# Attention block on one core: DVE's and TensorE's first tiles reordered, image work put ahead of the maxima, six stores issued from ACT's queue

## The reference

```
h    = group_norm(x, 32 groups of 4 channels) * gamma + beta      # (C, N)
q, k, v = w_qkv @ h + b_qkv                                       # each (C, N)
attn = softmax(q^T k / sqrt(C))                                   # (N, N)
out  = x + w_proj @ (attn @ v)^T + b_proj
```

## Time and profile before

| | |
|---|---|
| Median of 3 runs | 129.59 us (128.44 to 129.79) |
| The profiled execution | 127.29 us |
| Its span in the trace | 125.5 us |
| TensorE (PE) busy | 114.0 us, 91% |
| DVE busy | 96.1 us, 77% |
| ACT busy | 90.8 us, 72% |
| POOL busy | 87.4 us, 70% |
| Granted clock of TensorE | 0.999 of full |
| Data moved by DMA | 20.66 MB in 67,728 packets |

### The profile page before, as it was taken

One profiled execution on the slowest core, in us unless ns is written; L12 is line 12 of the kernel. 1 busy time (PEld: TensorE's weight loads), 2 busy tenths in 40 slices (PEclk: granted clock), 3 DMA queues, 4 the chain that ended last, 5 costly groups with the idle time before them and its releaser, 6 DMA issues.

```text
span 125.5 us, 3198 instructions
## 1 busy us (share of the span) xinstructions
PE 114.0 (91%) x1193; PEld 79.2 (63%) x1193; DVE 96.1 (77%) x240; ACT 90.8 (72%) x126; POOL 87.4 (70%) x73
## 2 busy tenths in 40 slices
PE   5987976869999999999999999999999999998981
PEld 2442544547767777666656776776567867776970
DVE  3688799999776967988669579775695887776832
ACT  3039499499987878777897878878878788788200
POOL 2054079489999998999759988998666666766000
PEclk9999999999999999999999999999999999999999
DMA  4594007968889998999999999999999999999602
GB/s 112 140 341 161 0 4 133 174 116 166 167 60 205 194 179 145 239 193 190 132 261 195 140 202 235 193 139 213 214 173 124 208 230 196 123 209 227 168 5 84
DMA packets 67728, 20.66 MB, mean 165 GB/s; under 512 B 65409, under 2 KB 66177, under 8 KB 67713
## 3 DMA queue, kind: packets, MB, share of 16 engines
q1 hardware_dynamic: 67280, 20.46, 87.2%
q10 hardware_dynamic: 432, 0.00, 0.2%
HBM read 2.36 MB, written 2.10 MB: 36 GB/s over the span
## 4 chain that ended last, share of the span: by engine, by line
PE 71%; DVE 10%; POOL 6%; issue 4%; DMA 4%; ACT 3%; POOLq 0%; DVEq 0%
PE scores L743 10%; PE o_ps L761 10%; PE scores L745 10%; PE scores L744 10%; PE o_ps L769 10%; PE o_ps L762 9%; DVE row_max L539 4%; DMA ptT<-p_hl 4%; POOL p_hl L342 3%; PE scores L787 3%; PE o_ps L782 2%; DVE t_lo L527 2%; ACT z_hi L406 1%; PE misc L728 1%; PE misc L727 1%
## 5 line engine op out<-in xcount | busy, mean ns | idle before, releaser
L342 POOL TENSOR_TENSOR p_hl<-probs,p_hl 128x1024 f16<-128x1024 f32 x31 | 66.1, 2135 | 13.7 <-ACT p_hl L432 13.6
L539 DVE TENSOR_REDUCE row_max<-scores 128x1 f32<-128x1024 f32 x32 | 39.1, 1221 | 17.2 <-PE scores L745 17.0
L425 ACT ACTIVATE probs<-scores,exp_bias,esc 128x1024 f32<-128x1024 f32 x32 | 38.5, 1203 | 14.6 <-DVE exp_bias L544 14.6
L432 ACT ACTIVATE p_hl<-probs 128x1024 f16<-128x1024 f32 x32 | 33.8, 1057 | 1.0
L761 PE MATMUL o_ps<-v_hi,ptT 128*128 128x128 f16 x256 | 32.0, 219 | 1.7 <-issue 1.3
L762 PE MATMUL o_ps<-v_lo,ptT 128*128 128x128 f16 x256 | 32.0, 219 | 0.0
L761 PEld LDWEIGHTS o_ps<-v_hi,ptT 128*128 128x128 f16 x256 | 24.9, 98 | 8.2 <-issue 6.0
L743 PE MATMUL scores<-z_hi,t_hi 128*128 128x512 f16 x64 | 24.3, 379 | 2.6 <-ACT probs L425 1.7
L762 PEld LDWEIGHTS o_ps<-v_lo,ptT 128*128 128x128 f16 x256 | 25.0, 98 | 2.3
L745 PE MATMUL scores<-z_hi,t_lo 128*128 128x512 f16 x64 | 24.2, 379 | 0.0
L744 PE MATMUL scores<-z_lo,t_hi 128*128 128x512 f16 x64 | 24.2, 379 | 0.0
(11 more groups left out here) (134 smaller groups left out, 138.4 us busy)
## 6 DMA issues: line engine op xcount, KB each, us to landing
out_dram<-out_sb SPq DMA_DIRECT2D x7, 256.0 KB, 2.6
x_sb<-in_x_dram SPq DMA_DIRECT2D x3, 512.0 KB, 4.5
ptT<-p_hl SPq DMA_TRANSPOSE x61, 3.4
x_sb<-in_x_dram SPq DMA_DIRECT2D x2, 256.0 KB, 3.2
out_dram<-out_sb SPq DMA_DIRECT2D x1, 192.0 KB, 2.0
wqkv_sb<-in_L_conv_w_qkv_dram SPq DMA_DIRECT2D x1, 128.0 KB, 3.7
wp_sb<-in_L_conv_w_proj_dram SPq DMA_DIRECT2D x1, 64.0 KB, 3.4
wqkv_sb<-in_L_conv_w_qkv_dram SPq DMA_DIRECT2D x1, 64.0 KB, 3.1
```

The source lines that it names most:

```text
L342: nc.gpsimd.tensor_tensor(p_hl[:, g % RING, 1], probs[:, g % RING], p_hl[:, g % RING, 0], ALU.subtract).then_inc(plo_ready, 1)
L425: nc.scalar.activation(probs[:, g % RING], scores[:, g % SLOTS], ACT.Exp, bias=exp_bias[:, g:g + 1], scale=esc[:], accum_out=row_sum[:, g: ...
L432: nc.scalar.activation(p_hl[:, g % RING, 0], probs[:, g % RING], ACT.Copy).then_inc(phi_ready, 1)
L539: nc.vector.tensor_reduce(row_max[:, g:g + 1], scores[:, g % SLOTS], AX_X, ALU.max).then_inc(max_ready, 1)
```

## The change

The computation stays the same. The edits:

1. `store` becomes a helper with the queue as an argument. The six stores of tiles 0 to 23 are issued by ACT, in its loop behind `p_high(g)` at g = 9, 13, ..., 29. SP keeps the transposes and the last three stores.
2. `score_tile` at the first tile of an image waits for `thi_ready` first and for `tlo_ready` only ahead of the first matmul that reads `t_lo`.
3. Tile 0: on DVE `w_max` and `w_inv` come ahead of `t_low(0, 1)`, on TensorE the matmul for `w_max` comes ahead of `t_products(0, 1)`.
4. The copy to `ident16` moves from tile 2 to the prologue, ahead of the wait for gamma.
5. Image 1: `group_mean(1)` moves on DVE ahead of maxima(3), `group_var(1)` and `v_low(0, ...)` behind it; `normalise(1, ...)` on POOL and `z_high(1, ...)` on ACT move one tile later, from tiles 2 and 3 to 3 and 4. Statistics of image 2: `channel_stats` at tiles 4 and 5, TensorE's `group_mean(2)` at tile 6.
6. On DVE `t_low(b, 1)`, `v_low`, `channel_stats`, `group_mean`, `group_var` of the later images stand ahead of the maxima; `t_low(b + 1, 0)` stands directly behind the maxima of the image's last tile.
7. `v_products` and `v_high` of images 1 to 3 run at tiles s = 0 and 1 instead of 1 and 2. `values` waits for each half of `v_lo` only where it first reads it.

```diff
--- before.py
+++ after.py
@@ -251,6 +251,12 @@
 
         block = ctx.enter_context(nc.Block())
 
+        def store(queue, first, tiles):
+            b, s = divmod(first, TILES)
+            queue.wait_ge(out_ready, first + tiles)
+            queue.dma_start(out_d[b, :, s * P:(s + tiles) * P],
+                            out_sb[:, first * P:(first + tiles) * P]).then_inc(stored, 16)
+
         @block.sync
         def _(sp):
             w_d = w_qkv.rearrange("(t o) c -> o t c", t=3)
@@ -266,12 +272,6 @@
             for b in range(1, B):
                 sp.dma_start(x_sb[:, b * N:(b + 1) * N], x_d[b]).then_inc(x_rest[b - 1], 16)
 
-            def store(first, tiles):
-                b, s = divmod(first, TILES)
-                sp.wait_ge(out_ready, first + tiles)
-                sp.dma_start(out_d[b, :, s * P:(s + tiles) * P],
-                             out_sb[:, first * P:(first + tiles) * P]).then_inc(stored, 16)
-
             for g in range(G):
 
                 wait(sp, pv_ready, g - PT_RING + 1)
@@ -283,13 +283,9 @@
                     sp.wait_ge(plo_ready, g + 1)
                     sp.dma_start(ptT[:, g % PT_RING, 1], p_hl[:, g % RING, 1], transpose=True
                                  ).then_inc(lo_transposed[g % RING], 16)
-                done = g - LAG - CT - 1
-                if done >= 0 and done % CT == 0:
-                    store(done, CT)
-            for first in range(G - 2 * CT, G - CT, CT):
-                store(first, CT)
-            store(G - CT, CT - 1)
-            store(G - 1, 1)
+            store(sp, G - 2 * CT, CT)
+            store(sp, G - CT, CT - 1)
+            store(sp, G - 1, 1)
             sp.wait_ge(stored, 16 * (G // CT + 1))
 
         @block.gpsimd
@@ -376,9 +372,8 @@
                 if g == 1:
                     power(1)
                     shift(1)
-                if g in (2, 3):
-                    normalise(1, g - 2)
                 if g in (3, 4):
+                    normalise(1, g - 3)
                     z_low(1, g - 3)
 
                 if s == 7 and b + 2 < B:
@@ -459,13 +454,17 @@
                 b, s = divmod(g, TILES)
                 exponentials(g)
                 p_high(g)
+
+                done = g - LAG - CT - 1
+                if done >= 0 and done % CT == 0:
+                    store(act, done, CT)
                 if g == 1:
                     v_high(0, 0)
                     v_high(0, 1)
-                if s in (1, 2) and b >= 1:
-                    v_high(b, s - 1)
-                if g in (2, 3):
-                    z_high(1, g - 2)
+                if s in (0, 1) and b >= 1:
+                    v_high(b, s)
+                if g in (3, 4):
+                    z_high(1, g - 3)
                 if s in (6, 7) and b + 1 < B:
                     t_high(b + 1, s - 6)
 
@@ -501,6 +500,7 @@
             nc.vector.tensor_scalar(group_avg[:].rearrange("p (g j) -> p g j", j=GROUP),
                                     group_sum[:].unsqueeze(2).broadcast_to([P, P // GROUP, GROUP]),
                                     1.0 / GROUP, None, ALU.mult).then_inc(const_dve, 1)
+            nc.vector.tensor_copy(ident16[:], ident32[:]).then_inc(ident16_ready, 1)
             dve.wait_ge(gcol_loaded, 16)
             nc.vector.tensor_scalar(g_diag[:], ident32[:], gamma_c[:], None, ALU.mult).then_inc(gdiag_ready, 1)
 
@@ -630,11 +630,25 @@
                     scale_output(done)
                 if done >= 1:
                     add_input(done - 1)
+
+                if s == 1 and b >= 1:
+                    t_low(b, 1)
+                if s in (2, 3) and b >= 1:
+                    v_low(b, s - 2)
+                if s in (4, 5) and 1 <= b < B - 2:
+                    channel_stats(b + 2, s - 4)
+                if s == 6 and b + 2 < B:
+                    group_mean(b + 2)
+                if s == 7 and b + 2 < B:
+                    group_var(b + 2)
+                if g == 3:
+                    group_mean(1)
                 maxima(g)
+                if s == 7 and b + 1 < B:
+                    t_low(b + 1, 0)
                 if g >= 1:
                     inverse_sum(g - 1)
                 if g == 0:
-                    t_low(0, 1)
                     dve.wait_ge(wmax_psum, 1)
                     nc.vector.tensor_reduce(w_max[:, 1:2], o_ps[:, 1, 2 * P:3 * P], AX_X, ALU.max).then_inc(wmax_all, 1)
                     dve.wait_ge(wmax_all, 1)
@@ -642,31 +656,20 @@
                                             ).then_inc(wmax_safe, 1)
                     dve.wait_ge(wmax_safe, 1)
                     nc.vector.reciprocal(w_inv[:], w_max[:, 2:3]).then_inc(winv_ready, 1)
+                    t_low(0, 1)
                 if g == 1:
                     channel_stats(1, 0)
                     channel_stats(1, 1)
                 if g == 2:
-                    nc.vector.tensor_copy(ident16[:], ident32[:]).then_inc(ident16_ready, 1)
                     dve.wait_ge(bo_psum, 1)
                     dve.wait_ge(o_loaded, 32)
                     nc.vector.tensor_tensor(bo[:], bp_c[:], o_ps[:, 0, 0:1], ALU.add).then_inc(bo_ready, 1)
-                    group_mean(1)
+                if g == 3:
+                    group_var(1)
                     v_low(0, 0)
-                    group_var(1)
                     v_low(0, 1)
-                if s in (2, 3) and b >= 1:
-                    v_low(b, s - 2)
-                if b + 2 < B:
-                    if s in (3 if b == 0 else 1, 4):
-                        channel_stats(b + 2, s // 4)
-                    if s == 5:
-                        group_mean(b + 2)
-                    if s == 6:
-                        group_var(b + 2)
-                if s == 7 and b + 1 < B:
-                    t_low(b + 1, 0)
-                if s == 0 and b >= 1:
-                    t_low(b, 1)
+                if g in (4, 5):
+                    channel_stats(2, g - 4)
 
 
             scale_output(LAST - 4)
@@ -730,7 +733,11 @@
 
             def score_tile(g):
                 b, s = divmod(g, TILES)
-                pe.wait_ge(tlo_ready, t_part(b, s // CT) if g else 1)
+
+                if s == 0:
+                    pe.wait_ge(thi_ready, t_part(b, 0) if b else 1)
+                else:
+                    pe.wait_ge(tlo_ready, t_part(b, s // CT))
                 wait(pe, exp_ready, g - SLOTS + 1)
                 if s == 0:
                     pe.wait_ge(zlo_ready, b * 2 + 2 if b else 1)
@@ -742,6 +749,8 @@
                     dst = scores[:, g % SLOTS, half * HALF:(half + 1) * HALF]
                     nc.tensor.matmul(dst, t_hi[:, rows], z_hi[:, cols], start=True, stop=False)
                     nc.tensor.matmul(dst, t_hi[:, rows], z_lo[:, cols], start=False, stop=False)
+                    if s == 0 and half == 0:
+                        pe.wait_ge(tlo_ready, t_part(b, 0) if b else 1)
                     last = nc.tensor.matmul(dst, t_lo[:, rows], z_hi[:, cols], start=False, stop=True)
                 last.then_inc(scores_ready, 1)
 
@@ -753,9 +762,10 @@
                     pe.wait_ge(hi_moved, g - LAST + 2)
 
                 wait(pe, out_ready, g - 1)
-                pe.wait_ge(vlo_ready, b * 2 + 2)
                 dst = o_ps[:, g % 2, 0:P]
                 for k in range(TILES):
+                    if g % TILES == 0 and k % CT == 0:
+                        pe.wait_ge(vlo_ready, b * 2 + k // CT + 1)
                     keys = slice(b * N + k * P, b * N + (k + 1) * P)
                     hi = ptT[:, g % PT_RING, 0, k]
                     nc.tensor.matmul(dst, hi, v_hi[:, keys], start=(k == 0), stop=False)
@@ -828,11 +838,15 @@
             for g in range(G):
                 b, s = divmod(g, TILES)
                 score_tile(g)
+
+                if g == TILES - 2:
+                    pe.wait_ge(vlo_ready, 1)
+                    group_mean(2)
                 if g == 0:
-                    t_products(0, 1)
                     pe.wait_ge(wdiag_ready, 1)
                     nc.tensor.matmul(o_ps[:, 1, 2 * P:3 * P], onesb[:], w_diag[:], start=True, stop=True
                                      ).then_inc(wmax_psum, 1)
+                    t_products(0, 1)
                 if g == 1:
                     pe.wait_ge(wraw_ready, 1)
                     pe.wait_ge(o_loaded, 32)
@@ -849,9 +863,9 @@
                     for half in range(2):
                         pe.wait_ge(tlo_ready, t_part(0, half))
                         v_products(0, half)
-                if s in (1, 2) and b >= 1:
-                    pe.wait_ge(tlo_ready, t_part(b, s - 1))
-                    v_products(b, s - 1)
+                if s in (0, 1) and b >= 1:
+                    pe.wait_ge(tlo_ready, t_part(b, s))
+                    v_products(b, s)
 
                 if g == 3:
                     group_mean(1)
@@ -859,8 +873,7 @@
                     for _ in range(KEEP_WARM):
```

(3 more changed lines are left out.)

## The result

The changed kernel took 125.03 us (median of 4 runs, 124.04 to 126.86), the kernel before 129.05 us in the same comparison (4 runs, 128.44 to 129.79). The ratio is 0.966, with a 95% interval of 0.956 to 0.976: faster, and inside the predicted range (122.4 to 127.2), 0.8 us above the predicted 124.2. Medians here are over all executions, while a ratio compares only those within 1.5% of the fastest of their kernel, so it need not be the ratio of the medians. The profiled execution took 124.99 us with a span of 123.2, where before had 127.29 and 125.5. So the profiled executions differ by 2.3 us and the medians by 4.0.

What follows compares the result with a forecast made beforehand. TensorE was taken as the bound from tile 8 on, before that a chain through DVE, POOL and ACT. Start 2.9 + gaps 2.7 - new waiting 0.6 + end 0.4 = 5.4 us; 129.59 - 5.4 = 124.2 us, range 122.4 to 127.2.

Steps and rivals of the forecast that it cites:

- Score tile 0: First score tile starts on t_hi without waiting for t_lo; all that follows 0.4 us earlier, bounds 0.35 and 0.43.
- w_max, cast and tiles 2 to 8: Earlier w_max and cast, reordered image 1 work; with tile 0's gain, tile 8 starts 2.9 us earlier, bounds 1.2 and 3.1.
- The gaps: Tiles 8 to 31: TensorE's short idle times between tiles go, 2.74 us in all, bounds 1.5 and 2.74.
- The allowance: Tiles 9 to 15: 0.6 us of new waiting for transposes, bounds 0 and 1.8.
- the tightest place: Tile 12, low half of tile 8: transposes' spare time of 1.5 us falls to 0.35 us.
- Stores on ACT: Six stores leave SP, 4.0 us of its issue time; cost on ACT 0, showing above about 2 us per store.
- The end: Low half of tile 30 lands sooner without a store ahead of it: 0.4 us gained, bounds 0 and 0.49.
- SP's queue: SP's unbroken transpose issues start 2.0 us earlier while TensorE reaches tile 12 3.15 us earlier, leaving 0.35 us spare.
- "slower" rival: ACT's stores slip between packets of SP's transposes and hold them up: 3.2 us slower, 132.8 us; chance 0.05.
- The range: Whole kernel: measured time between 122.4 and 127.2 us.
- first rival: Transposes become the bound from tile 12 on: gain only about 3 to 3.5 us, 126.3 us; chance 0.18.

Runs made afterwards that it cites:

- e0: The changed kernel once more, unaltered, in a second comparison: 125.44 us, ratio 0.973 to the kernel before.
- e11: The kernel before with only DVE's cast to ident16 moved ahead of the wait for gamma's load: 126.76 us, ratio 0.986 to the kernel before.
- e9: The changed kernel with the cast to ident16 back at tile 2: 127.67 us, ratio 0.988 to the kernel before.
- e5: The changed kernel without the six stores of the loop (output lacks those tiles): 124.12 us, ratio 0.956 to the kernel before.
- e6: The changed kernel with three of the six loop stores issued from SP behind the last transpose: 123.49 us, ratio 0.962 to the kernel before.
- e10: The changed kernel with all six loop stores moved behind the last transpose on SP: 122.59 us, ratio 0.954 to the kernel before.
- e8: The changed kernel with six dummy matmuls on TensorE ahead of values of tile 29: 125.63 us, ratio 0.978 to the kernel before.
- e12: The kernel before with its six loop stores moved behind the last transpose on SP: 128.44 us, ratio 0.998 to the kernel before.
- e2: The kernel before with only the six stores moved to ACT's queue: 129.01 us, ratio 1.003 to the kernel before.
- e1: The changed kernel with the six stores back in SP's loop: 127.14 us, ratio 0.989 to the kernel before.
- e3: The kernel before with only the new loop order of images 1 to 3, old start, stores on SP: 128.71 us, beside 128.29 before.
- e4: The kernel before with only the new first tiles, early cast and tile 0's t_hi wait: 126.48 us, ratio 0.986 to the kernel before.

## Why the prediction was right, and where it was not

The forecast for the start counted from tile 0 at 11.56 to tile 8 at 34.6, 23.04 us; the trace has 23.21.

- **Score tile 0** starts 0.30 us after the start of the last `t_products` matmul (12.07 to 12.37) instead of 0.68 (11.27 to 11.95), so the 0.4 us are there. They don't show in its start, 12.37 against a forecast of 11.56: the 0.8 us came from the prologue ahead of it, where TensorE's granted clock stood at 0.50 for 3.4 us (last section). In e0 it stood at 1.00, and tile 0 starts at 11.65.
- **w_max, cast and tiles 2 to 8.** Counted from tile 0, POOL's first `p_low` starts at 5.54 us (forecast 16.97 - 11.56 = 5.41, before 5.93), tile 5 at 12.95 (forecast 13.04, before 15.22), and the last `z_lo` ends at 22.26 (forecast 22.14, before 23.48). The cast was 0.22 us long, as the Trainium skill's rule has it, not the 1.8 of its length alone; e11 and e9 show it as the largest single part.
- **The gaps.** 2.74 us were forecast. Where no transpose is late (e5, e6, e10) tiles 8 to 31 take 70.16 us, 2.79 less than before. In the changed kernel 0.64 of that is lost to transposes: a gap of 0.36 us while tile 15 runs, one of 0.27 while tile 29 does. The allowance was 0.6, for tiles 9 to 15. The sum of this stretch, 70.81, is met by 70.80, in part by luck: at tile 12, "the tightest place", TensorE waited for nothing, and the same loop took 70.67 us in e0 and 71.81 in e8.
- **Stores on ACT.** Nothing waits behind them on ACT, as forecast, and an issue takes 0.34 us of ACT instead of the 0.6. But the prediction had the step only as an issue taken off SP. Its other side, the landings of the transposes beside them (median 4.0 instead of 3.4 us for low halves), was only in the rivals.
- **The end is the step that failed.** The prediction had "0.49 us off TensorE's wait" for the low half of tile 30, and took -0.4. That wait did go, but tile 29's high half took its place with 2.0 us, a low half before it with 0.6, and the end grew by 1.8 us. Its reading of the wait was wrong too: it put the landing of 4.7 us down to the store ahead of that transpose, and in e5, e10 and e12, with no store ahead of it, the same transpose took 4.9, 4.7 and 4.8 us. The main error is in the step before, *SP's queue*: its spare time was worked out at tile 12, where the start's gain had just come in on both sides (3.15 us of TensorE, 2.0 of SP). From there TensorE gains 1.9 us more by the gaps and SP nothing. The tight place is the last one, and the same sum made there would have shown a wait of about 1 us. Before, the high half of tile 29 landed 3.3 us after 111.26, and TensorE in score tile 31's stretch needed it some 2 us later than that; TensorE was to be over 5 us earlier, SP about 2. In the trace they are 4.1 and 1.8 us earlier, which leaves about 0.3 us of wait by this sum; the other 1.7 came from the landing, for which the prediction had no term at this place. The "slower" rival had even counted the transposes down to tile 29, with an issue at 106.1; it came at 110.75, since the pace from `lo5` on was 1.54 us, not 1.46 (74.0 us for 48).

- **The range.** Its good side takes 6.7 us off. The bounds named there, 3.1, 2.74 and the end's 0.49, make 6.3. The measured time lies far from that side.

So the first rival, the transposes as the bound, came true at the last three tiles. It was priced at 126.3 for all that lay behind tile 13; the measured 125.03 is between it and the forecast. Counted in profiled executions, the forecast span was 120.1 us and the measured one 123.2: 0.8 by tile 0's start, 0.2 by tiles 0 to 8, 2.2 by the end. In e0, where tile 0 starts at 11.65, the span is 121.8, and the 1.7 us above the forecast are those of the end. Against medians the miss is smaller (5.4 us forecast, 4.0 measured), since the profiled execution before started score tile 0 at 11.95, early for its kind (e2 and e12, with the same prologue: 14.09 and 14.14).

Why did tile 29's high half take 5.0 us to land? In the changed kernel's DMA view from 109.4 to 114.4 (kind: packets, MB, share of 16 engines) an instruction load stands beside the transposes:

```profile
q1 hardware_dynamic: 3023, 0.75, 106.8%
q8 instruction: 1, 0.02, 2.0%
```

It is one packet, in work from 111.86 to 113.49. The windows of the same trace, while TensorE waits, show that the other transfers were nearly done by then (last two numbers: DMA share and GB/s of packets that start in the window):

```profile
112.90:113.40 0.50, 0.00 (x0) 0.00 (x0) 0.50 (x2) 0.00 (x0) 0.00 (x0) 1.00 0.00 0
113.50:114.40 0.90, 0.00 (x0) 0.00 (x0) 0.81 (x1) 0.00 (x0) 0.00 (x0) 1.00 0.27 52
```

For 0.5 us no packet starts at all, though three transposes are on their way, and they go on once the load is done. In six of the fourteen traces such a q8 load began two microseconds or more before this transpose had landed (after, e0, e1, e3, e8, e9), and the landing took 4.7 to 5.2 us; in the eight others it took 3.3 or 3.4. There are 854 of these transposes in the fourteen traces. Between issue and landing 479 of them had an instruction load (q8 or q14) in work, and 207 of those took 4.3 us or more (median 4.2); of the 375 without one, 4 did (median 3.3). The kernel before has the same: all 12 of its long landings had a load beside them. (A longer flight also has more room to meet a load.) In e6 the transpose had landed 0.6 us before the load began. So the late queue seems to have cost TensorE its lateness and, on top, a meeting with the load. No run moved a load by itself: the link is shown by counting, not by an experiment, and what places the loads stays open.

## What to carry to other kernels

When an engine's gaps are closed, work out for every queue that feeds it how much further ahead the queue gets, and do that sum at the last item, not at the first tight one. Here a gain at the head moved the queue by nearly as much (1.8 of 2.0 us), a gain spread over the loop by 0.8 of 2.8.

Transfers that nobody waits for (plain stores of results) belong behind those that somebody waits for. Moving them to another engine's queue was worth nothing by itself here; moving them behind the last transpose was worth another 1.2 to 1.9% once the transposes were the limit, and nothing measurable before that.

A small cast on DVE beside a long GpSimd instruction can cost that instruction's length: look at the same operation's shortest and longest times in the trace.

## What was not expected of the hardware

- TensorE's clock fell to 0.50 of full for some 3 us after it had idled 2.31 and 2.28 us close to the end (e1, e3), and stayed at 1.00 after 2.01 and 2.11 us (the changed kernel, e0). A wait there can be paid twice.
- Transposes on their way beside an instruction load landed late in 207 of 479 cases (4.3 us or more), the others in 4 of 375.
- The prologue's length differs between executions of kernels with the same prologue, by TensorE's rate in it. Score tile 0 started between 11.62 us (e6) and 14.07 us (e1), all with the new order of the start. The six warm-up matmuls ahead of it span 2.19 us in the changed kernel, 1.46 in the kernel before and 2.77 in e1:

```profile
9.55 2.19 PE L797 MATMUL scores<-warm,ones 128*128 128x512 f16 x6
```

```profile
8.86 1.46 PE L787 MATMUL scores<-warm,ones 128*128 128x512 f16 x6
```

```profile
10.23 2.77 PE L796 MATMUL scores<-warm,ones 128*128 128x512 f16 x6
```

In the changed kernel the granted clock had fallen to 0.50 there, and in the kernel before it had not (windows of the two, in this order; the clock is the number before the last two):

```profile
7.60:11.00 3.40, 3.40 (x12) 1.59 (x12) 2.85 (x10) 2.12 (x5) 2.87 (x7) 0.50 0.94 352
```

```profile
7.60:11.00 3.40, 2.73 (x17) 1.23 (x15) 2.86 (x11) 2.44 (x6) 2.84 (x7) 1.00 0.89 347
```

Ahead of that fall TensorE had been idle for 0.60 us, waiting for a load of weights, a wait that the kernel before did not have; so the idle times of the first point are no rule. The profiled executions of the new start fall into three groups: tile 0 at 11.62 to 11.79 us (e6, e0, e9; clock 1.00), at 12.31 to 12.47 (e4, e10, the changed kernel, e8; 0.50 for 3.4 us in the prologue), and at 13.84 and 14.07 (e5, e1). In the last group the matmuls run at half the rate until about 14 us, though the views print 1.00: the trace has no record of the clock before that.

This spread of 2.5 us is as large as one of the change's gains. A single pair of profiled executions can't tell it from an effect of the change, and stretches cut at score tiles can: tiles 0 to 8 take 23.19 to 23.23 us in all profiled executions with the same start (the changed kernel, e0, e1, e5, e6, e8 and e10).
